# A decoder of two layers on one core: two norm applications and a quantisation in another order on DVE

## The reference, cut to what matters

```
x = layernorm(x + L0_attn(x))          # causal attention, 16 heads of 16, quantised k and v, LoRA
x = layernorm(x + L0_xattn(x, ctx))    # cross attention over 77 keys, 16 heads of 16
x = layernorm(x + L0_ffn(x))           # act_quant, ternary weights, depthwise conv, silu
x = layernorm(x + L1_attn(x))          # tanh recurrence over the sequence
x = layernorm(x + L1_xattn(x, ctx))    # cross attention, 16 heads of 64
x = layernorm(x + L1_ffn(x))           # layernorm, act_quant, w1, gelu, layernorm, act_quant, w2

def act_quant(x):                      # in front of both products of an ffn
    scale = 127 / clip(max(abs(x), axis=-1), 1e-5)
    return clip(round(x * scale), -128, 127) / scale
layernorm(x) = (x - mean) / sqrt(var + 1e-5)
```

## Time and profile before

| | us |
|---|---|
| median of 3 executions | 2236.44 |
| lowest, highest | 2230.43, 2236.94 |
| profiled execution, its own time | 2234.12 |
| profiled execution, span | 2232.1 |

### The profile page before, as it was taken

The page is one execution under the profiler, slowest core; times in us unless marked ns, Lnnn a source line. Parts: engine busy times, 40 slices in busy tenths (PEclk is TensorE's granted clock), DMA queues, the critical chain, the costliest instruction groups (busy, mean ns, idle before and its releaser), DMA issues. The chain is left out here.

```text
span 2232.1 us, 36088 instructions
## 1 busy us (share of the span) xinstructions
PE 1726.7 (77%) x11992; PEld 1068.5 (48%) x11992; DVE 1745.6 (78%) x4446; ACT 1379.1 (62%) x3471; POOL 888.6 (40%) x983
## 2 busy tenths in 40 slices
PE   7789999999977778775567775547499999955665
PEld 4333333333345666664445554435266667723333
DVE  4788888888637888887878888874378878769997
ACT  1116666666733434433078888889999996246665
POOL 2431000000018886655233433310286686534443
PEclk9898999999979988996668887776699999967766
DMA  2101111111021000000000000001000000010000
GB/s 74 49 13 26 30 28 28 31 31 28 13 68 34 13 10 13 13 6 1 1 15 20 1 1 1 1 1 36 24 1 20 1 1 1 1 36 17 17 20 19
DMA packets 42488, 41.29 MB, mean 18 GB/s; under 512 B 16044, under 2 KB 34352, under 8 KB 42304
## 3 DMA queue, kind: packets, MB, share of 16 engines
q1 hardware_dynamic: 42303, 39.00, 6.5%
HBM read 21.79 MB, written 4.19 MB: 12 GB/s over the span
## 5 line engine op out<-in xcount | busy, mean ns | idle before, releaser
L823 ACT ACTIVATE ST<-ST,aexp 128x1 f32<-128x1 f32 x2046 | 583.2, 385 | 2.4 <-PEq L58 2.4
L623 ACT ACTIVATE PT<-PS 128x512 f32<-128x512 f32 x576 | 309.8, 597 | 153.3 <-PE PS L374 122.1
L514 DVE CUSTOM_DVE_ANT_0 junk<-PS,maskw 128x128 bf16<-128x128 f32 (+3 forms) x512 | 226.8, 486 | 27.9 <-PE PS L351 27.8
L351 PE MATMUL PS<-KT,QT 48*128 48x512 bf16 (+3 forms) x768 | 180.3, 337 | 33.1 <-DVE MX L514 17.9
L517 DVE TENSOR_REDUCE MX<-PS 128x1 f32<-128x512 f32 x256 | 164.5, 684 | 30.0 <-PE PS L351 27.1
L395 PE MATMUL PS<-PT,VP 128*32 128x256 f32 (+1 forms) x2560 | 184.2, 370 | 0.0
L95 PE MATMUL PS<-ident,X 128*128 128x128 f32 x256 | 61.6, 328 | 134.9 <-DVE X L142 131.1
L673 POOL TENSOR_SCALAR nm<-MX 128x16 f32<-128x16 f32 x32 | 6.5, 204 | 377.6 <-DVE MX L520 377.6
L1500 DVE SCALAR_TENSOR_TENSOR U<-U,f_cw 128x128 f32<-128x128 f32 x512 | 152.4, 370 | 0.0
L1773 PE MATMUL PS<-Y,l_pT 128*128 128x256 f32 (+1 forms) x640 | 143.7, 379 | 2.7 <-issue 2.7
L1757 PE MATMUL PS<-Q,l_xT 128*128 128x512 f32 (+1 forms) x384 | 143.9, 525 | 1.7 <-DVE l_s L1807 1.7
(11 more groups left out here) (315 smaller groups left out, 4404.6 us busy)
## 6 DMA issues: line engine op xcount, KB each, us to landing
KT<-KS SPq DMA_DIRECT2D x192, 32.0 KB, 2.0
QT<-QS SPq DMA_DIRECT2D x192, 32.0 KB, 2.0
X<-in_x SPq DMA_DIRECT2D x8, 512.0 KB, 3.7
Y<-in_x SPq DMA_DIRECT2D x32, 128.0 KB, 2.0
out<-j_xn SPq DMA_DIRECT2D x32, 128.0 KB, 1.7
QT<-NMT SPq DMA_DIRECT2D x192, 2.0 KB
U<-in_L_ffn_w SPq DMA_DIRECT2D x2, 1024.0 KB, 6.8
j_raw<-in_L_ffn_w SPq DMA_DIRECT2D x2, 1024.0 KB, 4.9
```

Of the source, the lines that this page charges most:

```text
L351: T.matmul(bank(u % 3)[:, 0:w * P], QT[i % R][rows, qt * P:(qt + 1) * P], KT[i % R][rows, k0 * P:(k0 + w) * P], start=True, stop=True).the ...
L514: V.tensor_tensor_reduce(junk[u % 3][:, 0:w * P], bank(u % 3)[:, 0:w * P], maskw[:, BANK - w * P:], 1.0, NEG, ALU.add, ALU.max, MX[i % 2][ ...
L623: C.activation(PT[n % 4][:, 2 * pr + e, 0:w], bank(3 + u % 3)[:, 0:w], ACT.Exp, scale=0.25).then_inc(e_done, 1)
L823: C.activation(self.ST[:, m, t:t + 1], self.ST[:, m, t - 1:t] if t else self.zero[:, :], ACT.Tanh, bias=self.BU[:, m, t:t + 1], scale=self ...
```

## The change

Two places in DVE's lists change; no instruction is added, taken out or altered, and the other engines' lists stay as they are.

1. In cross attention 0 the applications of norms C and D come behind the quantisation of a slot. The quantisation, of a tile whose norm was applied one slot earlier, comes first.
2. In the last stage the application of the last norm to tile j - 4, so far the end of slot j, is done in slot j + 1, behind L1977. The loop has one slot more.

```diff
         def dve_cross(j):
             p, sc, c, q, o = j - 5, j - 4, j - 1, j - 8, j - 6
-            if on(c - 1):
-                nC.dve_apply(c - 1, X[:, c - 1, :], cx[(c - 1) % 3][:, :]).then_inc(c_xn, 1)
-            if on(o - 1):
-                nD.dve_apply(o - 1, X[:, o - 1, :], X[:, o - 1, :]).then_inc(d_xn, 1)
             if on(q):
                 V.wait_ge(d_xn, q + 1)
...
                 qE.dve_round(q, eq[q % 2][:, :], et[q % 2][:, :]).then_inc(e_xq, 1)
+            if on(c - 1):
+                nC.dve_apply(c - 1, X[:, c - 1, :], cx[(c - 1) % 3][:, :]).then_inc(c_xn, 1)
+            if on(o - 1):
+                nD.dve_apply(o - 1, X[:, o - 1, :], X[:, o - 1, :]).then_inc(d_xn, 1)
             if on(p):
                 V.wait_ge(d_exp, p + 1)
...
-            for j in range(NT + 4):
-                b, c, d, e = j - 1, j - 2, j - 3, j - 4
+            for j in range(NT + 5):
+                b, c, d, e, z = j - 1, j - 2, j - 3, j - 4, j - 5
                 if on(b):
...
                     V.scalar_tensor_tensor(h[b % 3][:, :], bank(1 + 2 * (b % 2), 2), ds[:, b:b + 1], bh[:, :], ALU.mult, ALU.add).then_inc(j_h, 1)
+                if on(z):
+                    if z >= 4:
+                        V.wait_ge(out_st[z % 4], landed(z - 4, 4))
+                    n3.dve_apply(z, xn[z % 4][:, :], y[z % 2][:, :]).then_inc(n_xn, 1)
                 if on(d):
...
                     V.scalar_tensor_tensor(hn[c % 3][:, :], hn[c % 3][:, :], rs[c % 3][:, :], b2_[:, :], ALU.mult, ALU.add).then_inc(j_l2b, 1)
-                if on(e):
-                    if e >= 4:
-                        V.wait_ge(out_st[e % 4], landed(e - 4, 4))
-                    n3.dve_apply(e, xn[e % 4][:, :], y[e % 2][:, :]).then_inc(n_xn, 1)
```

## The result

| | before | changed |
|---|---|---|
| median, us | 2233.69 (6 runs, 2230.43 to 2236.94) | 2176.88 (6 runs, 2174.47 to 2182.69) |
| profiled execution, own time / span, us | 2234.12 / 2232.1 | 2175.48 / 2173.8 |

The account below looks back on a forecast made before the run. It took DVE's rings to bound both stages, with waits for POOL's `nC_rs` and `n_rs`; 20 us in cross attention 0 plus 14 in the last stage made 34, taking the median from 2236.44 to 2202 us, range 2180 to 2226.

Parts of the forecast that it names:

- What bounds the kernel: Cross attention 0: DVE and POOL's ring, DVE waiting 38.3 us for `nC_rs`; last stage: DVE waiting 13.6 us for `n_rs`.
- Part 2, the rings: Cross attention 0: quantisation fits under the 1.58 us wait; DVE and POOL's ring falls from 11.03 to 9.60 us.
- L770 slots: Cross attention 0: four slots with a 2.82 us POOL step, whose scale and copy steps move ahead of it; gain 7.1 us.
- the prediction's own rules: Cross attention 0: start times for row sums, multiply, subtraction and next application; 274.5 us in the old order, trace 275.6.
- The step that failed: Both stages: TensorE's clock stays in its present mix, granted 0.90 in cross attention 0 and 0.73 in the last stage.
- The term for cross attention 0: Quantisation ahead of the norm applications in 24 slots gains 20 us: 10.5, 2.7 and 7.1 by kind of slot.
- the ring of ACT and TensorE: Last stage: at 7.28 us on average it outlasts DVE's 6.96 and limits the gain to 14 us.
- B: Both stages: TensorE's clock rises, chains shorten, gains of 34 and 22 us give 2180 us; chance 0.17.
- C: Cross attention 0: quantisation is held up beside POOL's powers, its part brings 5 to 8 us; 2216 us, chance 0.16.
- D: Both stages: chains run at the low clock in the shortened slots, nearly no change; 2232 us, chance 0.11.
- E: Last stage: TensorE stays at 1.2 GHz, its ring with ACT takes 8.17 us; slower, 2245 us, chance 0.05.
- At nothing: Tail end unchanged, slots from 33 on only reordered, last stage's L1977 not stretched beside `j_xb`: each 0 us.

Follow-up runs that it names:

- e3: Kernel before the change, with extra identity transposes where TensorE stood idle in cross attention 0 and the last stage: 2230.40 us.
- e4: Changed kernel with its last-stage edit taken back, so only cross attention 0 is reordered: 2200.52 us, 0.9849 of the kernel before.
- e5: Changed kernel with its cross attention 0 edit taken back, so only the last stage is reordered: 2206.61 us, 0.9882 of the kernel before.
- e2: Changed kernel with constant-tile row sums on DVE, about 1.4 us a slot in cross attention 0 and 0.9 in the last stage: 2228.06 us.
- e6: Changed kernel with constant-tile row sums on DVE, about 0.7 us a slot in cross attention 0 and 0.45 in the last stage: 2200.29 us.
- e7: Changed kernel with constant-tile row sums on DVE, about 0.3 us a slot in cross attention 0 and 0.2 in the last stage: 2186.87 us.
- e1: Changed kernel with extra identity transposes in TensorE's chains, 11 a slot in cross attention 0 and 9 in the last stage: 2217.13 us.
- e8: Changed kernel with POOL's two bias sums moved in cross attention 0, so norm applications meet no POOL work: 2169.22 us, 0.9712 of the kernel before.

## Why the prediction was wrong

**What bounds the kernel.** Right in both stages. DVE's ring with the quantisation behind the wait, and the wait for `n_rs`, were the bounds. That taking them away shortened the slots shows it, and e3 shows that TensorE's chains were not the bound before: a high clock left the slots as they were.

**Part 2, the rings.** Right, and to the tenth in the slots without a weight step. The quantisation fits under the wait, row sums come 1.48 us after C, and the ring of DVE and POOL has 9.60 us. The four L770 slots (11, 12, 17 and 18) gained 8.8 us where 7.1 were said; slots 17 and 18 went from 12.51 and 12.52 us to 10.00 and 10.05. Stepping through slots 8 to 31 with the prediction's own rules, but with the 24 chains as the changed kernel's trace has them (two of 5.3 and two of 5.15 us, none after slot 15; else 4.0 to 4.2), gives about 243 us; the trace has 243.8 (C of slot 8 at 707.23, of slot 32 at 951.06). With the chains of the kernel before the same rules give some 10 us more, the 254 of the forecast.

**The step that failed** is the assumption under the forecast, that TensorE's clock stays in its present mix (granted 0.90 and 0.73); it rose to 0.97 and 0.84. Before there were 12 long chains (5.2 us and more) in 24 slots, now there are 4 (5.15 and more). The term for cross attention 0 was sized 20 us and measured 33 (e4). Most of the difference lies in the 13 slots without a weight step, all of them now behind a short chain: they were to gain 10.5 us and gained 19.6. The seven slots with a weight step of 3.7 us gained 3.3, where 2.7 were said. The same assumption made the ring of ACT and TensorE the next bound of the last stage, 7.28 us on average. The changed kernel's trace shows this ring at either clock. Three stretches in a row, each from one `j_hqT` (L2041) to the next, in the order of the earlier trace rows, and the two `j_hqT` not shown above:

```profile
2084.72:2092.54 7.82, 5.23 (x21) 3.17 (x22) 7.65 (x15) 5.00 (x8) 4.71 (x5) 0.56 0.05 17
2092.54:2098.88 6.34, 3.29 (x22) 2.06 (x22) 6.17 (x14) 5.01 (x9) 3.23 (x4) 1.00 0.07 22
2098.88:2105.21 6.33, 3.29 (x22) 2.06 (x22) 6.16 (x13) 5.00 (x9) 3.22 (x4) 1.00 0.06 22
```

```profile
2098.88 1.11 ACT L2041 ACTIVATE j_hqT<-PS,j_down 128x1024 bf16<-128x1024 f32 x1
...
2105.21 1.11 ACT L2041 ACTIVATE j_hqT<-PS,j_down 128x1024 bf16<-128x1024 f32 x1
```

With the clock at 1.00 throughout the ring takes 6.33 us, with 0.56 it takes 7.82. Most of the stage is this group of three, 20.49 us against three slots of DVE, 20.61. So the ring is no longer than DVE's, but hardly shorter either, and all slots have DVE's 6.87 us. This term was sized 14 us and measured 26 (e5); 0.09 us a slot, 2.5 us in all, is also that DVE's ring came out at 6.87 and not at 6.96. Together some 58 us instead of 34.

**The rivals.** B was the right one, 2180 us against 2177, and had 0.17. That it came so close is in part luck: of its two parts the first was 34 us, where 33 were measured, the second 22, where 26 were. What spoke for it, less idle time on TensorE, was in the text; against it I had set that the work grows by only 7% of the time, with no row to say what 7% does. The runs e2, e6 and e7 now say it: in the last stage 0.71 at 7.73 us, 0.77 at 7.33, 0.81 at 7.06. C did not come: scale 0.35 and copy 0.24 us beside the powers. The Trainium skill (GPSIMD Engine Reference, the table of specifications) says that POOL shares its SBUF interfaces with VectorE and contends with DVE instructions in a two-port performance mode or with two SBUF inputs. The applications agree, with 0.82 us beside POOL's sums and 0.41 without; beside the powers the only stretched row was POOL's own, the power at 0.66 us. That DVE's scale step caused it is argued from their overlap, not shown. D's mechanism is real: e1, which lengthens the chains as a low clock would, leaves 16 of the 57 us. E isn't tested, since no run holds the clock low throughout; nor does one show what the new order would have taken with the clock held at 0.90 and 0.73. But E's length of the ring, 8.17 us, was right: in six slots of e2 and e6 one `j_hqT` follows the other after 8.15 us, with the clock at 0.50.

**The range** ended at B's own time and had no room below it. B's numbers are sums of two rounded parts, and the median of the kernel before was itself 2.7 us lower in six runs than in three. The lower end should have been B less its own uncertainty.

**At nothing** I had put the tail, the slots from 33 on, and L1977 beside `j_xb`. The marks at 1064 and 1564 us agree, and L1977 takes 1.28 us there against 1.27 before.

## What to carry to other kernels

When a chain through TensorE is the next bound, don't price it at the clock that the trace of the old order shows. Here shorter slots left TensorE idle for less of the time, the clock rose, the chain got shorter, and the gain fed itself. Take the chain at both clocks (6.33 and 8.15 us in the last stage), and give the high one real weight where the change cuts TensorE's idle time. And look for independent steps of the same engine that stand behind a wait: moving them in front of it is worth their full length, until the next ring is reached, which can be worked out from the same trace.

## What the runs showed of the hardware that I had not expected

The granted clock answers to the slot's length within a stage, independently of other stages: 0.73, 0.77, 0.81 and 0.84 for slots of 7.79, 7.33, 7.06 and 6.87 us with the same TensorE work, with a scatter of about 0.03 (0.70 for 7.79 us in e4). A power of 128 x 1 elements on POOL does not hold up a scale step of DVE beside it (0.35 us), while a sum of 128 x 256 elements doubles an application (0.82 against 0.41 us in e8).
